# Local block: the feed-forward's layer norm on token rows

## The reference, cut to what matters

```python
for i in range(DEPTH):                      # DEPTH = 6
    x = attn_layer(shift_tokens(x), Wqkv[i], q_scale[i], k_scale[i], Wo[i]) + x
    x = ffn_layer(shift_tokens(x), ln_g[i], ln_b[i], W1[i], b1[i], W2[i], b2[i]) + x

def ffn_layer(x, g, bln, W1, b1, W2, b2):
    mu = x.mean(-1, keepdims=True)
    var = ((x - mu) ** 2).mean(-1, keepdims=True)
    xn = (x - mu) / jnp.sqrt(var + 1e-05) * g + bln
    hg = xn @ W1 + b1
    a, gate = jnp.split(hg, 2, -1)
    return a * jax.nn.gelu(gate, approximate=False) @ W2 + b2
```

## Time and profile before

| | |
|---|---|
| median of 3 runs | 4304.2 us (4294.06 to 4309.1) |
| the profiled execution | 4290.83 us, span 4289.1 us |
| mean granted clock of PE | 0.976 |
| busy, share of the span | PE 4007.8 us (93%), DVE 3256.0 (76%), POOL 2944.0 (69%), ACT 2597.3 (61%) |

### The profile page before, as it was taken

One profiled execution on the slowest core, in us unless ns is written; L12 is line 12 of the kernel. 1 busy time (PEld: TensorE's weight loads), 2 busy tenths in 40 slices (PEclk: granted clock), 3 DMA queues, 4 the chain that ended last, 5 costly groups with the idle time before them and its releaser, 6 DMA issues. The chain is left out here.

```text
span 4289.1 us, 151479 instructions
## 1 busy us (share of the span) xinstructions
PE 4007.8 (93%) x66856; PEld 2950.2 (69%) x66856; DVE 3256.0 (76%) x3915; ACT 2597.3 (61%) x3040; POOL 2944.0 (69%) x3505
## 2 busy tenths in 40 slices
PE   8989969999999999999878887799999999999998
PEld 5655557787777787877633333677778777777775
DVE  4535568887888888888668884788888888887885
ACT  4525436666667667667537774466666666666664
POOL 2202168888888888888534441788888888888884
PEclk9999989999999999999989998899999999999999
DMA  4304233233333323322100000333323333232221
GB/s 154 123 10 155 96 100 85 72 88 83 80 84 86 82 76 90 89 66 76 40 11 1 1 1 8 113 81 81 87 79 85 85 85 86 75 87 75 75 65 41
DMA packets 169725, 316.93 MB, mean 74 GB/s; under 512 B 39336, under 2 KB 43056, under 8 KB 166640
## 3 DMA queue, kind: packets, MB, share of 16 engines
q1 hardware_dynamic: 153520, 241.18, 20.7%
q0 software_dynamic: 15552, 66.07, 5.0%
HBM read 92.03 MB, written 20.05 MB: 26 GB/s over the span
## 5 line engine op out<-in xcount | busy, mean ns | idle before, releaser
L694 PE MATMUL psum<-loc_w_hl,loc_z_lo 128*128 128x512 f32 x1152 | 510.0, 443 | 32.5 <-DMA loc_w_hl<-parted 25.9
L941 ACT ACTIVATE loc_sq<-psum 128x1024 f32<-128x1024 f32 x192 | 196.6, 1024 | 459.7 <-PE psum L696 454.6
L1187 DVE TENSOR_REDUCE loc_ssq<-loc_sq 128x16 f32<-128x1024 f32 x384 | 464.1, 1208 | 4.5 <-POOL loc_rn L1076 4.5
L1080 POOL TENSOR_TENSOR loc_rc_k<-loc_rc_k,loc_rs_k 128x1024 f32<-128x1024 f32 x192 | 454.2, 2366 | 19.0 <-DVE loc_rs_k L1201 19.0
L695 PE MATMUL psum<-loc_w_hl,loc_z_hi 128*128 128x512 f32 x1152 | 456.9, 397 | 2.2 <-issue 2.0
L696 PE MATMUL psum<-loc_w_hl,loc_z_hi 128*128 128x512 f32 x1152 | 457.2, 397 | 0.0
L1080 POOL TENSOR_TENSOR loc_rc_q<-loc_rc_q,loc_rs_q 128x1024 f32<-128x1024 f32 x192 | 456.8, 2379 | 0.0
L1099 POOL TENSOR_TENSOR loc_prob<-loc_prob,loc_recip 128x1024 f32<-128x1024 f32 x192 | 365.5, 1904 | 92.1 <-DVE loc_recip L1224 90.5
L791 PE MATMUL psum<-loc_PT,loc_V 64*64 64x32 f32 x24576 | 405.1, 220 | 8.6 <-issue 8.0
L791 PEld LDWEIGHTS psum<-loc_PT,loc_V 64*64 64x64 f32 x24576 | 381.1, 135 | 34.7 <-issue 11.0
L1182 DVE TENSOR_TENSOR loc_rc_q<-psum,loc_rot 128x1024 f32<-128x1024 f32 x192 | 234.9, 1223 | 213.9 <-ACT loc_sq L936 184.0
(11 more groups left out here) (198 smaller groups left out, 9598.4 us busy)
## 6 DMA issues: line engine op xcount, KB each, us to landing
loc_V<-loc_V SPq DMA_DIRECT2D x1152, 128.0 KB
loc_V<-loc_V SPq DMA_DIRECT2D x672, 64.0 KB
loc_w_hl<-parted POOLq DMA_DIRECT2D x72, 512.0 KB, 4.4
parted<-moe_halves POOLq DMA_DIRECT2D x18, 1024.0 KB, 5.2
moe_spread<-moe_gates SPq DMA_DIRECT2D x64, 256.0 KB, 4.0
moe_raw<-in_wqkv POOLq DMA_DIRECT2D x18, 512.0 KB, 6.1
moe_w<-in_moe_w SPq DMA_DIRECT2D x32, 256.0 KB, 3.4
loc_wo<-in_wo SPq DMA_DIRECT2D x12, 512.0 KB, 4.9
```

Of the source, the lines that this page charges most:

```text
L694: pe.matmul(M.bank[bank + g], z_lo[:, r, tokens], w[:, 0, cols], start=True, stop=False)
L1080: pool.tensor_tensor(rc, rc, rs[:, :], ALU.add).then_inc(added, 1)
L1187: dve.tensor_reduce(ssq[:, a:a + HEADS], heads(sq[:, :]), AX_X, ALU.add).then_inc(totalled, 1)
```

## The change

The mean, the variance by matmuls and the spread go. PE transposes the residual of a sequence to token rows (turn_rows, four transposes into bank 6, behind v's projection in the step n % 4 == 0). DVE takes bn_stats and bn_aggr per tile from there (row_statistics, behind q's sum of squares). POOL adds epsilon, makes the inverse deviation as before, and the product lift = -mean x inverse deviation, in three operations more. ACT normalises the rows from bank 6 with that as scale and bias (norm_rows, four activations, behind the copy of the values in the step n % 4 == 1), PE transposes back (turn_back, bank 7, behind q's projection), and the affine reads that bank. Some waits for a bank to be free name other events, and entries of pe_passed and pool_passed are added.

```diff
-        xc, sqf, xn = sb("xc", [P, T]), sb("sqf", [P, T]), sb("xn", [P, T])
-        var, rstd, vt = (sb(n, [P, TILES]) for n in ("var", "rstd", "vt"))
+        rows, xn = sb("rows", [P, TILES, D]), sb("xn", [P, T])
+        halves, stats = sb("halves", [P, TILES, 6]), sb("stats", [P, TILES, 2])
+        var, rstd, vt, lift = (sb(n, [P, TILES]) for n in ("var", "rstd", "vt", "lift"))
...
                 if i == 0:
-                    pe.wait_ge(centred, upto_seq(L, s - 1))
+                    pe.wait_ge(hid_ready, upto_seq(L, s - 2, FBLK) - 1)
                 elif i == 1:
-                    pe.wait_ge(var_ready, upto_seq(L, s - 1))
                     pe.wait_ge(z_ffn, upto_seq(L, s - 2))
                 elif i == 2:
-                    pe.wait_ge(z_attn, upto(L, t - 1))
+                    pe.wait_ge(xn_ready, upto_seq(L, s - 1))
                 else:
                     pe.wait_ge(hid_ready, upto_seq(L, s - 1, FBLK) - 2)
+                pe.wait_ge(z_attn, upto(L, t - 1))
+                pe.sem_inc(pe_passed, 1)
                 for p in range(PAIRS):
                     mm = pe.matmul(M.bank[ZB][:, 0:P], wo[:, p, :], outT[:, p // (PAIRS // 2), p % (PAIRS // 2), :],
                                    start=(p == 0), stop=(p == PAIRS - 1))
                 mm.then_inc(y_full, 1)
 
-            def mean(L, t):
+            def turn_rows(L, t):
+                s = t // TILES
                 pe.wait_ge(z_attn, upto(L, t))
-                pe.wait_ge(hid_ready, upto_seq(L, t // TILES - 1, FBLK) - 1)
-                pe.matmul(M.bank[ZB], M.mean_w[:, :], zs[:, t // TILES % SEQS, 0:T], start=True, stop=True).then_inc(mean_full, 1)
-
-            def variance(L, t, newest):
-                pe.wait_ge(xc_squared, upto_seq(L, t // TILES))
-                pe.wait_ge(z_attn, upto(L, newest))
-                for i in range(TILES):
-                    mm = pe.matmul(M.bank[ZB][:, i * P:(i + 1) * P], sqf[:, i * P:(i + 1) * P], M.mean_w[:, :],
-                                   start=True, stop=True)
-                mm.then_inc(var_full, 1)
-
-            def spread(L, t):
-                s = t // TILES
-                pe.wait_ge(rstd_ready, upto_seq(L, s))
                 pe.wait_ge(hid_ready, upto_seq(L, s - 1, FBLK))
                 for i in range(TILES):
-                    mm = pe.matmul(M.bank[FB][:, i * P:(i + 1) * P], rstd[:, i:i + 1].broadcast_to([P, P]), M.ident[:, :],
-                                   start=True, stop=True)
-                mm.then_inc(spread_full, 1)
+                    mm = pe.transpose(M.bank[FB][:, i * P:(i + 1) * P], zs[:, s % SEQS, i * P:(i + 1) * P], M.ident[:, :])
+                mm.then_inc(rows_full, 1)
+
+            def turn_back(L, t, newest):
+                pe.wait_ge(rows_normed, upto_seq(L, t // TILES))
+                pe.wait_ge(z_attn, upto(L, newest))
+                pe.wait_ge(z_ffn, upto_seq(L, t // TILES - 1))
+                pe.sem_inc(pe_passed, 1)
+                for i in range(TILES):
+                    mm = pe.transpose(M.bank[ZB][:, i * P:(i + 1) * P], rows[:, i, :], M.ident[:, :])
+                mm.then_inc(back_full, 1)
 
...
-                if newest is not None:
-                    pe.wait_ge(var_ready, upto_seq(L, newest // TILES))
+                pe.wait_ge(z_attn, upto(L, newest))
...
-                if live(n - 6) and lasts(n - 6):
-                    spread(L, n - 6)
                 if live(n - 7) and lasts(n - 7):
                     gate(L, n - 7, 1)
                 if live(n):
                     project_v(L, n, live(n - 2))
+                if live(n - 5) and lasts(n - 5):
+                    turn_rows(L, n - 5)
+                if live(n):
                     project_q(L, n, live(n - 3))
-                if live(n - 5) and lasts(n - 5):
-                    variance(L, n - 5, newest)
+                if live(n - 6) and lasts(n - 6):
+                    turn_back(L, n - 6, newest)
...
-                    last_matmul(L, n - 9, n - 5 if live(n - 5) else None)
+                    last_matmul(L, n - 9, newest)
                 if live(n - 7) and lasts(n - 7):
                     gate(L, n - 7, 2)
-                if live(n - 4) and lasts(n - 4):
-                    mean(L, n - 4)
...
-            def square_centred(L, t):
-                act.wait_ge(centred, upto_seq(L, t // TILES))
-                act.activation(sqf[:, :], xc[:, :], ACT.Square).then_inc(xc_squared, 1)
+            def norm_rows(L, t):
+                act.wait_ge(norm_ready, upto_seq(L, t // TILES))
+                for i in range(TILES):
+                    done = act.activation(rows[:, i, :], M.bank[FB][:, i * P:(i + 1) * P], ACT.Identity,
+                                          scale=rstd[:, i:i + 1], bias=lift[:, i:i + 1])
+                done.then_inc(rows_normed, 1)
 
             def affine(L, t):
                 if t == TILES - 1:
                     act.wait_ge(norm_loaded, L * 16 + 16)
-                act.wait_ge(xn_scaled, upto_seq(L, t // TILES))
-                act.activation(xn[:, :], xn[:, :], ACT.Identity, scale=vec[:, 2 * FBLK + 1:2 * FBLK + 2],
+                act.wait_ge(back_full, upto_seq(L, t // TILES))
+                act.activation(xn[:, :], M.bank[ZB], ACT.Identity, scale=vec[:, 2 * FBLK + 1:2 * FBLK + 2],
                                bias=vec[:, 2 * FBLK + 2:2 * FBLK + 3]).then_inc(xn_ready, 1)
...
-                if live(n - 5) and lasts(n - 5):
-                    square_centred(L, n - 5)
...
+                if live(n - 6) and lasts(n - 6):
+                    norm_rows(L, n - 6)
                 if live(n):
                     copy_v(L, n)
...
-                step = L * (SEQS * 4) + s * 4
-                pool.wait_ge(var_ready, upto_seq(L, s))
+                step = L * (SEQS * 7) + s * 7
+                pool.wait_ge(stats_ready, upto_seq(L, s))
+                pool.tensor_scalar(var[:, :], stats[:, :, 1], LN_EPS, None, ALU.add).then_inc(rstd_step, 1)
+                pool.tensor_scalar(lift[:, :], stats[:, :, 0], -1.0, None, ALU.mult).then_inc(rstd_step, 1)
+                pool.wait_ge(rstd_step, step + 2)
+                pool.sem_inc(pool_passed, 1)
                 pool.tensor_tensor(rstd[:, :], var[:, :], minus_half[:, 0:TILES], ALU.pow).then_inc(rstd_step, 1)
-                pool.wait_ge(rstd_step, step + 1)
+                pool.wait_ge(rstd_step, step + 3)
                 pool.tensor_tensor(vt[:, :], rstd[:, :], rstd[:, :], ALU.mult).then_inc(rstd_step, 1)
-                pool.wait_ge(rstd_step, step + 2)
+                pool.wait_ge(rstd_step, step + 4)
                 pool.tensor_tensor(vt[:, :], vt[:, :], var[:, :], ALU.mult).then_inc(rstd_step, 1)
-                pool.wait_ge(rstd_step, step + 3)
+                pool.wait_ge(rstd_step, step + 5)
                 pool.sem_inc(pool_passed, 1)
                 pool.tensor_scalar(vt[:, :], vt[:, :], -0.5, 1.5, ALU.mult, ALU.add).then_inc(rstd_step, 1)
-                pool.wait_ge(rstd_step, step + 4)
-                pool.tensor_tensor(rstd[:, :], rstd[:, :], vt[:, :], ALU.mult).then_inc(rstd_ready, 1)
+                pool.wait_ge(rstd_step, step + 6)
+                pool.tensor_tensor(rstd[:, :], rstd[:, :], vt[:, :], ALU.mult).then_inc(rstd_step, 1)
+                pool.wait_ge(rstd_step, step + 7)
+                pool.tensor_tensor(lift[:, :], lift[:, :], rstd[:, :], ALU.mult).then_inc(norm_ready, 1)
...
-            def centre(L, t):
+            def row_statistics(L, t):
                 s = t // TILES
-                dve.wait_ge(mean_full, upto_seq(L, s))
-                dve.tensor_tensor(xc[:, :], zs[:, s % SEQS, 0:T], M.bank[ZB], ALU.subtract).then_inc(centred, 1)
-
-            def take_variance(L, t):
-                dve.wait_ge(var_full, upto_seq(L, t // TILES))
-                dve.tensor_scalar(var[:, :], M.bank[ZB].rearrange("p (i n) -> p i n", n=P)[:, :, 0], LN_EPS, None, ALU.add).then_inc(var_ready, 1)
-
-            def rescale(L, t):
-                dve.wait_ge(spread_full, upto_seq(L, t // TILES))
-                dve.tensor_tensor(xn[:, :], xc[:, :], M.bank[FB], ALU.mult).then_inc(xn_scaled, 1)
+                dve.wait_ge(rows_full, upto_seq(L, s))
+                for i in range(TILES):
+                    dve.bn_stats(halves[:, i, :], M.bank[FB][:, i * P:(i + 1) * P]).then_inc(row_stats, 1)
+                for i in range(TILES):
+                    dve.wait_ge(row_stats, (L * SEQS + s) * TILES + i + 1)
+                    mv = dve.bn_aggr(stats[:, i, :], halves[:, i, :])
+                mv.then_inc(stats_ready, 1)
...
-                if live(n - 6) and lasts(n - 6):
-                    rescale(L, n - 6)
...
-                if live(n - 5) and lasts(n - 5):
-                    take_variance(L, n - 5)
...
-                if live(n - 4) and lasts(n - 4):
-                    centre(L, n - 4)
+                if live(n - 5) and lasts(n - 5):
+                    row_statistics(L, n - 5)
```

(18 more changed lines are left out.)

## The result

The changed kernel takes 4279.95 us, the median of 5 runs (4274.32 to 4287.03), beside 4309.1 us for the kernel before (4294.06 to 4314.3, 5 runs). The ratio is 0.9945, with an interval of 0.9922 to 0.9967: 0.55% faster. The forecast was 4345 and slower. A repeat beside other runs of the kernel before gave 0.994 (0.992 to 0.996), so the change is small but clear of the spread.

The account below looks back on a forecast made before the run. The prediction took PE's queue to set the pace, with POOL under a microsecond behind a stop. Pair +6, clock +41 and drains -4 gave +43 us: 4334 from the execution, 4347 from the median, stated as 4345, range 4250 to 4405.

Parts of the forecast that it names:

- PE's saving: On PE's queue: 2.77 us less and 0.90 more, net 1.87 us per sequence, 90 us in all.
- The statistics: On DVE: four bn_stats at 0.28 and the bn_aggr at 0.2 take 1.9 us together, bounds 1.2 to 2.6.
- the lateness of 1.15: On POOL: the deviation starts 1.15 us later, behind DVE's statistics, bounds 0.5 to 1.85.
- POOL's longer deviation: On POOL: three more operations, their gaps and one more wait ahead of pow add 0.95 us, bounds 0.7 to 1.2.
- The sum for the pair: In the two steps holding the statistics: PE idles 2.2 us, the pair grows 1.0; less the mean's 0.87, +6 us in all.
- a room of 0.82: Before q's transposes: POOL ends q's scaling 0.82 us before PE starts them, the mean of four pairs.
- The clock: Behind PE's longer waits: the clock falls in half of 48 pairs at 1.7 us, 41 us, bounds 0 and 82.
- +43: Whole kernel: the forecast total in us, from +6 for the pair, +41 for the clock and -4 for the drains.
- The drains: At the end of the two blocks: each about 2 us shorter through fewer handoffs, -4 us, bounds 0 and -8.
- The first: Rival for the whole kernel: PE's saving passes through, 90 us less, 4214; chance 0.15.
- the second: Rival: the pair comes out even without clock falls, the mean's 0.87 remains, 42 us less, 4262; chance 0.13.
- The third: Rival: the clock falls in every pair, 82 us, giving 4388; chance 0.10.

Follow-up runs that it names:

- e1: The changed kernel with the row statistics moved on DVE from behind q's sum of squares to behind the reciprocal: 4269.34 us, ratio 0.9907.
- e2: As e1, with epsilon and the negative mean made on DVE behind bn_aggr, not on POOL: 4235.09 us, ratio 0.983; again 4222.38 us, 0.9839.
- e3: The changed kernel with only turn_rows moved from behind v's projection to behind q's: 4273.74 us, ratio 0.9925.
- e4: The kernel before the change with eight small idle products added at the end of POOL's deviation: 4286.54 us, ratio 0.9982.
- e6: e2 without the Newton step of the deviation, four POOL operations less: 4267.77 us, ratio 0.9945.
- e9: e6 with eight idle products added at the end of POOL's deviation: 4224.01 us, ratio 0.9841.
- e10: The kernel before the change with four fulfilled waits on PE's queue ahead of each group of projection matmuls: 4292.2 us, ratio 1.0004.

## Why the prediction was wrong

**What bounds the kernel.** "PE's queue sets the pace, and what it no longer has to do is gained" left out that this queue also waited for nobody: 57.6 us of stalls in scores and values, more than three times the 18.5 of the earlier trace rows.

**PE's saving.** Forecast 90 us, measured 71 as work. The mean's was right (42 and 40). Of steps 0 and 1 48 were forecast and 29 came; in step 0 the first matmul behind the four transposes holds the queue 0.32 us and not 0.23, the rest I did not trace.

**The statistics.** Forecast 1.9 us for the eight operations, bounds 1.2 to 2.6; they took 0.88 + 0.36, with ends that overlap 1.16. My price for bn_stats was right (283 ns), for bn_aggr a little high (153 ns); their sum "together 1.9 us" was not met because instructions of one kind follow each other at less than their own duration (0.88 for four of 283). And the lateness of 1.15 was too large. The 53.1 us that POOL now idles ahead of the deviation are, by my count, two waits of 19.9 us in the drains and 13.3 us in the 46 other sequences, 0.3 each; before, its 33.2 us of idle time ahead of pow were two waits of 16.6 us in the drains and none elsewhere. So the statistics hold POOL up by 0.3 us, not 1.15, and e1 gets 0.2 of these back.

**POOL's longer deviation.** Forecast 0.95, measured 1.05 (from the deviation's start to the end of q's scaling 12.13 us before and 13.18 after, medians over the sequences). Right, and e2 shows that it was the term that mattered.

**The sum for the pair.** POOL is 0.3 + 1.05 = 1.35 later and not 2.1; with PE 0.92 earlier and a room of 0.82 that is 1.45 us of wait. The room was read well: over 46 pairs of the trace its mean is 0.87. Measured: 43 pairs wait, 1.47 us each. The mechanism was right, its size a third less than forecast. The pair nonetheless grew by 1.3 us (62/48) where 1.0 was forecast, as less of PE's work went away in it and step 0 has more stalls, other waits and half clock than before.

**The clock: the step that failed.** "I take a fall in half of the 48 pairs: 24 x 1.7 = 41 us". Time at half clock in the local blocks went from 40 to 41 us, and in steps 1 and 2 from 29 to 14. Two things were wrong in it. The waits are shorter than the mean of 2.0 that I took: of the 43 in step 1, 10 are 1.8 us or longer. And only one of these was followed by half clock, beside all 3 of that length inside the scores, and all 6 in the kernel before. It is not that such a wait never costs the clock: in e3 7 of 13 were followed by half clock, in e1 4 of 10. I had taken the price from the one wait of the earlier trace rows that had a fall behind it. By itself this turns +43 into +2.

**The drains.** Forecast 4 us shorter together; in two executions of the changed kernel they are 1.3 us longer and 0.7 shorter (104.0 before, then 105.3 and 103.3, from the end of the last scores to the end of the block's work). The rows are what is late there: four waits for L971, 2.6 and 4.0 us in each drain. That ACT stage I had at nothing.

**The missing term.** The wait that the change adds at q's transposes takes stalls and half clock out of the next step: -38 us. No part of the forecast had it, and it alone makes the sign: +62 for the pair, -50 for step 3, -38 for step 2 are -26. e4 shows the term without the change, e6 and e9 take it away and put it back. In all three the wait was made or taken away by work on POOL; no run made it in another way or at another place, so what exactly in the wait does it is open.

**The rivals.** The first (all of PE's saving passes) and the second (half of it, 4262, by a POOL delay of 1.1 us) come nearest in time, but neither is what happened, as the wait is there. The third, a fall in every pair, is refuted: of the 43 waits in step 1 of the changed kernel one was followed by half clock, with 384 more transposes in all. The Trainium skill, "TensorE: Matmul & The Clock Gate", section "Part 4: PE-mode transpose", says that the full clock does not engage for transposes; these runs do not bear that out for transposes among matmuls, as the wait of 1.24 us at 3278.23 stands behind the transposes of k and is followed by those of q and of the probabilities, and the stretch behind it (columns as in the earlier trace rows) is granted 1.00 throughout:

```profile
3278.00:3283.00 5.00, 4.77 (x146) 3.54 (x148) 4.58 (x5) 3.63 (x5) 4.60 (x4) 1.00 0.52 130
```

Of what would show me wrong, the wait under 40 us did not occur; bn_stats and bn_aggr lasted just under 1.2 us; and the granted clock stayed as it was in the local blocks (over the whole span it went from 0.976 to 0.971, by half clock outside them). The last two were the true signs.

## What to carry to other kernels

Before idle time that a change adds is priced, look whether the busiest queue also has idle time that no engine causes (issue), and in which step: a short wait ahead of it may cost nothing, and removing one may cost more than it frees. Take the lateness of a stage from all its instances, not from one timeline, and divide a group's idle time by the number of its waits and not by its instances: POOL's 33.2 us before pow are two waits in the drains. Where a queue of small operations ends in a wait of the bound engine, as POOL's here, an operation moved off it was worth its full duration while the wait was long (e2) and less than nothing once it was short (e6, and e9 gives the time back).

## What the runs showed of the hardware

**Stalls end behind an instruction packet.** The traces hold the transfers that bring instructions: 529 packets of 16 KB on q8, 256 of PE's entries (matmuls, weight loads and waits) to a packet, and in the local blocks one each 6.3 us. By my count in the kernel before, every one of the 66 stalls in scores or values ends 1.1 to 1.6 us after the end of such a packet (median 1.37; for random moments the median is 3.1 and 90% lie between 0.3 and 8.6), and the packet ahead of a stall comes 9.1 us after the one before it, where others come after 4.8 (medians). In the 3 us ahead of a stall PE took 231 entries, against 122 on average: scores and values are its densest stretches. That PE runs out of instructions there is what these times suggest. What decides when a packet is asked for, and why the chip is late with just these, stays open: e10's dose was too small, and no run here moved the packets themselves. That the trade between waits and stalls exists is shown by e4, e6 and e9; that packets are its cause is argued from these times alone.

**A stall is more often followed by half clock than a wait of the same length.** My count over all fourteen traces, in the local blocks, of PE's idle times and those with half clock behind them:

```
idle time, us     inside the scores     at q's transposes, step 1
1.6 to 1.8                16 of 37                       0 of 52
1.8 to 2.0                16 of 30                      12 of 40
over 2.0                  31 of 43                        3 of 8
```

Idle times of 1.0 to 1.4 us, at any place, had it behind them in 2 of 263 cases. But q's transposes in step 3, with waits of 2.3 us and more at the start of each block, had it in 28 of 28, so the place alone does not decide. Why is open.

**Operations not in the trace before:** bn_stats on 128 float32 from PSUM 283 ns, bn_aggr of six values 153 ns, and an ACT activation of 128 columns from PSUM with a scale and a bias per row 462 ns where I had 350; four of these in a row take 1.50 us.
